# A gated attention block with a sign-weight FFN: squares of q and k folded to 64 rows before one turn, gates one step later

## The reference

```python
q, k, v = silu(xn @ Wq), silu(xn @ Wk), silu(xn @ Wv)
z, a, b = xn @ Wz, xn @ Wa, xn @ Wb
q, k, v = (causal_dwconv(t, w) for t, w in ...)     # 4 taps a channel
q, k = rope(q), rope(k)
q = q / maximum(norm(q), 1e-12); k = k / maximum(norm(k), 1e-12)   # over the 128 of a head
for s in range(4):
    attn = sum(q * lag(k, s)) / sqrt(128)
    out += (attn * sigmoid(lag(a, s) * b)) * lag(v, s)
s = (out * rsqrt(mean(out * out) + eps) * norm_w * silu(z)) @ Wout
hidden = relu((xn @ sign(up).T) * up_scale)
g = silu((hidden @ sign(down).T) * down_scale * output_scale)
y = x + s * g
```

## Time and profile before

| | us |
|---|---|
| median of 3 runs | 1365.18 (1363.66 to 1366.58) |
| the profiled execution | 1367.5 |
| its span in the trace | 1365.6 |
| PE busy in the span | 1342.8 (98%) |
| DVE busy | 985.0 (72%) |
| ACT busy | 745.5 (55%) |
| POOL busy | 361.6 (26%) |

### The profile page before, as it was taken

One profiled execution on the slowest core, in us unless ns is written; L12 is line 12 of the kernel. 1 busy time (PEld: TensorE's weight loads), 2 busy tenths in 40 slices (PEclk: granted clock), 3 DMA queues, 4 the chain that ended last, 5 costly groups with the idle time before them and its releaser, 6 DMA issues.

```text
span 1365.6 us, 23197 instructions
## 1 busy us (share of the span) xinstructions
PE 1342.8 (98%) x6824; PEld 1136.1 (83%) x6824; DVE 985.0 (72%) x1529; ACT 745.5 (55%) x2209; POOL 361.6 (26%) x508
## 2 busy tenths in 40 slices
PE   6999999999999999999999999998999999999998
PEld 5788888888888888888888888887888888888887
DVE  7898999989999899998999999995122223334432
ACT  5666666666666666566665666665543444432221
POOL 6134243343434333343333334333000000000001
PEclk9999999999999999999999999999999999999999
DMA  8233434334343433443433434335511101165544
GB/s 290 63 79 87 98 81 111 94 86 101 78 113 90 92 94 86 109 101 82 97 97 90 101 86 107 76 76 137 183 65 26 41 21 47 47 193 193 165 138 144
DMA packets 123419, 138.81 MB, mean 102 GB/s; under 512 B 30704, under 2 KB 67568, under 8 KB 123120
## 3 DMA queue, kind: packets, MB, share of 16 engines
q1 hardware_dynamic: 114160, 121.48, 31.1%
q0 software_dynamic: 9216, 16.78, 7.1%
HBM read 62.58 MB, written 25.30 MB: 64 GB/s over the span
## 4 chain that ended last, share of the span: by engine, by line
PE 96%; DMA 1%; DVE 1%; ACT 1%; POOL 1%; issue 0%; SPq 0%; POOLq 0%; DVEq 0%; ACTq 0%
PE bank L909 50%; PE bank L1411 12%; PE bank L1214 9%; PE bank L1201 8%; PE bank L962 4%; PE bank L984 4%; PE bank L973 4%; PE bank L950 2%; PE bank L899 1%; DMA sq_sum<-out_sq 1%; PE bank L886 0%; DMA up_raw<-in_x 0%; PE bank L925 0%; PE bank L117 0%; DVE y_k L753 0%
## 5 line engine op out<-in xcount | busy, mean ns | idle before, releaser
L645 ACT ACTIVATE bank<-bank 128x128 f32<-128x128 f32 x512 | 134.7, 263 | 92.1 <-PE bank L973 91.9
L753 DVE SCALAR_TENSOR_TENSOR y_q<-u_q,cw_q,y_q 128x512 f32<-128x512 f32 x192 | 144.2, 751 | 38.6 <-ACT y_q L610 31.1
L1190 DVE TENSOR_TENSOR hid_lo<-relu,hid_hi 128x512 fp32r<-128x512 f32 x64 | 44.3, 693 | 170.7 <-ACT hid_hi L1182 170.6
L753 DVE SCALAR_TENSOR_TENSOR y_k<-u_k,cw_k,y_k 128x512 f32<-128x512 f32 x192 | 145.2, 756 | 28.0 <-ACT y_k L610 21.1
L753 DVE SCALAR_TENSOR_TENSOR y_v<-u_v,cw_v,y_v 128x512 f32<-128x512 f32 x192 | 144.4, 752 | 6.9
L503 POOL TENSOR_TENSOR rq_win<-rq_win,const 128x32 f32<-128x32 f32 x64 | 27.5, 430 | 451.7 <-DMA rq_win<-rq_scratch 451.7
L487 POOL TENSOR_TENSOR rnorm<-norms,neg_half 128x8 f32<-128x8 f32 x64 | 111.9, 1749 | 9.9 <-POOL norms L483 8.9
L1178 ACT ACTIVATE relu<-bank,us_sb 128x512 f32<-128x512 f32 x64 | 44.1, 689 | 121.1 <-PE bank L1201 121.1
L1302 ACT ACTIVATE hid_hi<-o_raw 128x512 fp32r<-128x512 f32 x64 | 40.2, 630 | 115.9 <-PE bank L1411 97.0
L1362 DVE TENSOR_TENSOR hid_lo<-o_raw,hid_hi 128x512 fp32r<-128x512 f32 x64 | 43.8, 690 | 79.9 <-ACT hid_hi L1302 79.9
L1411 PE MATMUL bank<-x_hi,hid_hi 128*128 128x512 f32 x256 | 99.6, 389 | 0.0
(11 more groups left out here) (186 smaller groups left out, 3483.7 us busy)
## 6 DMA issues: line engine op xcount, KB each, us to landing
swapped_q<-y_q SPq DMA_DIRECT2D x128, 128.0 KB, 2.3
swapped_k<-y_k SPq DMA_DIRECT2D x128, 128.0 KB, 2.3
o_scratch<-o_buf SPq DMA_DIRECT2D x64, 256.0 KB, 2.5
sq_sum<-out_sq POOLq DMA_DIRECT2D x64, 256.0 KB, 3.4
o_raw<-o_scratch SPq DMA_DIRECT2D x64, 256.0 KB, 3.9
raw_q<-in_wq SPq DMA_DIRECT2D x16, 256.0 KB, 3.1
raw_k<-in_wk SPq DMA_DIRECT2D x16, 256.0 KB, 3.6
raw_v<-in_wv SPq DMA_DIRECT2D x16, 256.0 KB, 4.3
```

The source lines that it names most:

```text
L645: last = nc.scalar.activation(block_of, block_of, ACT.Square, accum_out=norms[:, g1 % 2, i * BC + b:i * BC + b + 1])
L753: nc.vector.scalar_tensor_tensor(y[n][:, g % 2, :], u[n][:, g % 2, i:i + CH], cw[n][:, bass.ds(h * TAPS + i, 1)], y[n][:, g % 2, :], ALU.m ...
L1190: nc.vector.tensor_tensor(hid_lo[:, j % HS, :], relu[:, j % 2, :], hid_hi[:, j % HS, :].bitcast(fp32), ALU.subtract).then_inc(hid_lo_done, 1)
```

## The change

The norms are made in another way. ACT squares q and k as they are, channels on the partitions: of q, rows 0 to 63 go into `fold` rows 0 to 63 and rows 64 to 127 into `other` rows 0 to 63; of k, in the same way, into rows 64 to 127. A transfer issued by POOL adds `other` to `fold`, so that 64 rows hold the squares of q and 64 those of k. PE turns `fold` alone, with four transposes, between the v and the z projection of the next step (`turn_fold`), and DVE sums each turned block over its two halves of 64 columns (`sum_fold`) into `norms`.

The fourth tap of v moves: DVE makes taps two and three, ACT makes the fourth as a scaled copy into `last_tap`, and a second accumulating transfer of POOL adds it to `y`. Only the very last step keeps the old way, and there DVE adds `other` to `fold` too.

`make_gates`, `gate_scores` and `mask_band` take the chunk of three steps before, not two, and the last two stand on DVE behind the taps of k, with `sum_fold` between them. `join_out` moves behind the rotation. POOL's step has the two new transfers first and the roots last. SP stores the roots behind the swaps. `fold`, `other` and `last_tap` lie in `down_raw`, so the FFN's first `down` weights are loaded after the last step instead of before the first. In the tail of the attention, the last two squares of the output get places of their own (`late_sq`), and the order of the work is another. The diff, cut to its core:

```diff
+    late_sq = [swapped["q"][:, i, :] for i in range(2)]
...
+    DVE_TAPS = {"q": 3, "k": 3, "v": 2}
+    last_tap = down_raw[:, 1, :, :]
+    fold, other = down_raw[:, 0, 0, :], down_raw[:, 0, 1, :]
...
-            if at := back(h, g, 1):
-                store_rq(at[1], c)
             for n in "qk":
                 wait(sp, conv_done[n], 3 * c + 3)
                 wait(sp, rope_done[n], 3 * (c - 1))
                 for to, frm in ((0, HALF), (HALF, 0)):
                     sp.dma_start(swapped[n][to:to + HALF, g % 2, :], y[n][frm:frm + HALF, g % 2, :]
                                  ).then_inc(swap_in[n][g % 2], 16)
+            if at := back(h, g, 1):
+                store_rq(at[1], c)
...
+        sp.wait_ge(turned_f, NC)
+        env["load_down"](sp, 0)
         store_rq(G - 1, NC)
-        load_rq(G - 2, NC)
-        load_rq(G - 1, NC, rq_last_in)
+        load_rq(G - 2, NC, rq_late_in[0])
+        sp.wait_ge(rq_joined, NC - 2)
+        load_rq(G - 1, NC, rq_late_in[1])
+        sp.wait_ge(last_tap_added, 16 * (NC - 1))
+        env["load_down"](sp, 1)
...
+        def add_last_tap(g1, c):
+            wait(pool, last_tap_made, c)
+            wait(pool, conv_done["v"], 2 * c)
+            wait(pool, turned_v, c - 1)
+            pool.sem_inc(last_tap_asked, 1)
+            nc.gpsimd.dma_start(y["v"][:, g1 % 2, :], last_tap[:, g1 % 2, :], accum_op=ALU.add
+                                ).then_inc(last_tap_added, 16)
+
+        def fold_squares(c):
+            wait(pool, squares_done, c)
+            pool.sem_inc(fold_asked, 1)
+            nc.gpsimd.dma_start(fold, other, accum_op=ALU.add).then_inc(folded, 16)
 
         def step(h, g):
             c = h * G + g
+            if at := back(h, g, 1):
+                fold_squares(c)
+                add_last_tap(at[1], c)
+            if at := back(h, g, 3):
+                make_gates(at[1], c - 3)
+            if at := back(h, g, 4):
+                add_squares(at[1], c - 4)
             if at := back(h, g, 1):
                 roots(at[0], at[1], c)
                 if is_start(h, g - 1):
                     pool.wait_ge(gate_done, 2)
                 gate_keys(at[0], at[1], c)
-            if at := back(h, g, 2):
-                make_gates(at[1], c - 2)
-            if at := back(h, g, 4):
-                add_squares(at[1], c - 4)
 
         schedule(pool, step)
...
+            if n == "v" and not is_end(h, g):
+                nc.scalar.activation(last_tap[:, g % 2, :], u["v"][:, g % 2, HALO:], ACT.Copy,
+                                     scale=cw["v"][:, bass.ds(h * TAPS + HALO, 1)]
+                                     ).then_inc(last_tap_made, 1)
...
-        def square_qk(g1, c):
-            wait(act, turned_qk, c)
-            wait(act, rnorm_done, c - 2)
-            for i, bank in enumerate((bank_tqv, bank_tk)):
-                for b in range(BC):
-                    block_of = bank[:, b * P:(b + 1) * P]
-                    last = nc.scalar.activation(block_of, block_of, ACT.Square,
-                                                accum_out=norms[:, g1 % 2, i * BC + b:i * BC + b + 1])
-            last.then_inc(norms_done, 1)
+        def squares(n, g, c):
+            own, far = (slice(0, HALF), slice(HALF, D)) if n == "q" else (slice(HALF, D), slice(0, HALF))
+            wait(act, conv_done[n], 3 * c + 3)
+            wait(act, turned_f, c)
+            nc.scalar.activation(fold[own, :], y[n][own, g % 2, :], ACT.Square)
+            last = nc.scalar.activation(other[own, :], y[n][far, g % 2, :], ACT.Square)
+            if n == "k":
+                last.then_inc(squares_done, 1)
...
-            if at := back(h, g, 1):
-                square_qk(at[1], c)
             if not is_start(h, g):
                 silu_and_tap("q", bank_qv, h, g, c)
                 silu_and_tap("k", bank_kz, h, g, c)
             if g == 3 and not is_last(h):
                 split_hi("q", h + 1, c)
+            squares("q", g, c)
...
                 ffn.up_signs(1)
+            squares("k", g, c)
...
-        square_qk(G - 1, NC)
         square_out(NC - 4)
         silu_z(G - 2, NC - 2, bank_kz)
         copy_v(G - 1, NC)
-        save_spill(G - 3, NC)
-        silu_z(G - 1, NC - 1, bank_qv)
-        ffn.down_signs(0)
-        ffn.down_signs(1)
         for n in "qk":
             act.wait_ge(rope_done[n], 3 * NC)
         ffn.hidden(0, 0)
+        save_spill(G - 3, NC)
+        silu_z(G - 1, NC - 1, bank_qv)
         square_out(NC - 3)
         ffn.hidden(0, 1)
+        ffn.down_signs(0)
         save_spill(G - 2, NC + 1)
         ffn.hidden(0, 2)
-        square_out(NC - 2)
+        square_out(NC - 2, late_sq[0])
+        ffn.down_signs(1)
+        save_spill(G - 1, NC + 2)
         ffn.hidden(0, 3)
-        save_spill(G - 1, NC + 2)
         act.wait_ge(o_done, NC)
         ffn.up_signs(2)
         ffn.down_signs(2)
-        square_out(NC - 1)
+        square_out(NC - 1, late_sq[1])
...
+        def sum_fold(g1, c):
+            wait(dve, turned_f, c)
+            wait(dve, root_done, c - 2)
+            nc.vector.tensor_reduce(norms[:, g1 % 2, :].rearrange("p (n b) -> p b n", b=BC),
+                                    bank_tk[:, :].rearrange("p (b n d) -> p b n d", b=BC, n=2),
+                                    AxisListType.X, ALU.add).then_inc(norms_done, 1)
...
+            if at := back(h, g, 3):
+                gate_scores(at[1], c - 3)
+            if at := back(h, g, 1):
+                sum_fold(at[1], c)
+            if at := back(h, g, 3):
+                mask_band(at[1], c - 3)
...
-            conv_tap("v", 3, h, g, c)
+            if is_end(h, g):
+                conv_tap("v", 3, h, g, c)
+                dve.wait_ge(squares_done, NC)
+                nc.vector.tensor_tensor(fold, fold, other, ALU.add).then_inc(folded_last, 1)
...
-            if at := back(h, g, 2):
-                gate_scores(at[1], c - 2)
             if at := back(h, g, 3):
+                join_out(at[1], c)
                 make_o(at[0], at[1], c - 3)
             if g == 1 and not (isinstance(h, int) and h == 0):
                 split_lo("z", h)
-            if at := back(h, g, 2):
-                mask_band(at[1], c - 2)
...
         def turn_v(g1, c):
-            wait(pe, norms_done, c)
-            wait(pe, conv_done["v"], 3 * c)
+            wait(pe, v_tok_done, c - 1)
+            if isinstance(c, int) and c == NC:
+                pe.wait_ge(conv_done["v"], 2 * NC + 1)
+            else:
+                wait(pe, last_tap_added, 16 * c)
...
-        def turn_qk(g1, c):
-            wait(pe, v_tok_done, c - 1)
+        def turn_fold(c):
             wait(pe, norms_done, c - 1)
-            for n, bank in (("q", bank_tqv), ("k", bank_tk)):
-                wait(pe, conv_done[n], 3 * c)
-                for b in range(BC):
-                    last = nc.tensor.transpose(bank[:, b * P:(b + 1) * P],
-                                               y[n][:, g1 % 2, b * P:(b + 1) * P], ident)
-            last.then_inc(turned_qk, 1)
+            if isinstance(c, int) and c == NC:
+                pe.wait_ge(folded_last, 1)
+            else:
+                wait(pe, folded, 16 * c)
+            for b in range(BC):
+                last = nc.tensor.transpose(bank_tk[:, b * P:(b + 1) * P], fold[:, b * P:(b + 1) * P], ident)
+            last.then_inc(turned_f, 1)
...
-            if at1:
-                turn_qk(at1[1], c)
...
+            if at1:
+                turn_fold(c)
...
-        turn_qk(G - 1, NC)
         wait(pe, z_done, NC - 2)
         project("z", bank_kz, H - 1, G - 2, NC - 2)
+        turn_fold(NC)
         turn_v(G - 1, NC)
         wait(pe, silu_done["v"], 2 * NC)
         project("z", bank_qv, H - 1, G - 1, NC - 1)
+        pe.wait_ge(norms_done, NC)
+        ffn.up(0, 0)
+        score(G - 2, NC - 2)
         sum_values(G - 3, NC)
-        score(G - 2, NC - 2)
-        ffn.up(0, 0)
         pe.wait_ge(z_done, NC - 1)
```

More of the change, by code:

```diff
@@ L294, in attention @@
     swap_in = {n: [sem(f"swap_in_{n}{i}") for i in range(2)] for n in "qk"}
-    turned_qk = sem("turned_qk")
+    squares_done = sem("squares_done")
+    fold_asked = sem("fold_asked")
+    folded = sem("folded")
+    folded_last = sem("folded_last")
+    turned_f = sem("turned_f")
     turned_v = sem("turned_v")
@@ L304, in attention @@
     rq_in = sem("rq_in")
-    rq_last_in = sem("rq_last_in")
+    rq_late_in = [sem(f"rq_late_in{i}") for i in range(2)]
     rq_masked = sem("rq_masked")
@@ L335, in is_start, with is_end @@
         return isinstance(h, int) and h == 0 and g == 0
+    def is_end(h, g):
+        return is_last(h) and g == G - 1
     def is_last(h):
@@ L498, in make_gates @@
             win = rq_win[:, g2 % 2, :, :]
[L499 to L500 removed]
+            if isinstance(k, int) and k >= NC - 2:
+                pool.wait_ge(rq_late_in[k - NC + 2], 16)
             else:
@@ L512, in make_gates, with add_squares @@
```

(17 more changed lines are left out.)

42 lines of the change are left out of this document (25 added, 17 removed).

## The result

The changed kernel takes 1354.16 us (median of 4 runs, 1352.64 to 1355.98); the kernel before, on the same chip, 1365.86 (4 runs, 1363.66 to 1366.58). The ratio is 0.9921 [0.9909, 0.9933]: 0.8% faster, where 1338 was forecast. The profiled execution took 1355.53 us, its span 1353.7, against 1367.5 and 1365.6.

The account below looks back on a forecast made before the run. PE, busy 98% of the span, was taken as the bound. 1367.5 - 27.9 (transposes) + 4 (mask waits) - 3.2 (end) - 1.5 (first steps) = 1338.9, or 1336.6 against the median; it said 1338, range 1330 to 1355.

Parts of the forecast that it names:

- The slack of an ordinary step: Mask before `sum_values` in an ordinary step: PE able to start at about 11.6, due at 11.89, keeping 0.3 us.
- 16 x 0.25 = +4 us: Step after g = 3: three weight splits make DVE's mask late, PE waits about 0.25 us in each of 16 heads.
- at worst 0.9: Gates' loop through POOL, SP and DRAM: ready at 20.7, due at 23.1; slack 2.4 us, 0.9 with the slowest landing.
- The first steps: Start of the attention: one wait of 1.6 for `v_tok` goes, as the fold's turn no longer opens the step; -1.5 us.
- The end: End of the attention: idle time and half clock, together 6.7 us, go; three short pauses, 3.5 together, come; net -3.2.
- no half clock expected: End of the attention: the new pauses, 3.5 us together, would be too short to lower PE's granted clock.
- The two other pauses that were expected: End of the attention: about 1 us for late gates after `up(0, 0)`, and some 0.5 at the last `sum_values`.
- The mask is late in every step: Rival, DVE in the loop: reduce or its waits cost 0.9 to 1.1, not 0.62; 1354 us at 1.0; chance 0.13.
- reduce slow: Rival, DVE's reduction: a strided read at half rate takes 1.3 us, giving 1377, slower than before; chance 0.05.
- The gates' loop becomes the period: Rival, POOL, SP and DRAM: two more transfers double every landing, the loop passes 14.05 us, kernel slower; chance 0.03.
- No wait at all: Rival, the loop: taps start earlier and PE never waits for the mask; 1333 us; chance 0.10.
- the rival whose cause was not at work: The late mask in every step, with a reduce of 1.0 us: 1354, to which the range was widened; chance 0.13.

Follow-up runs that it names:

- e3: Changed kernel with VectorE's reduction made twice, the first result to a tile nobody reads: 1379.82 us, ratio 1.0098 to the kernel before.
- e6: Changed kernel with VectorE's program written out for all 16 heads, same operations and order: 1347.75 us, ratio 0.9878 to the kernel before.
- e12: Kernel before the change with VectorE's program written out and nothing else: 1365.28 us, ratio 0.9993 to the kernel before.
- e4: Changed kernel with the transfer adding v's fourth tap cut to 16 of 512 columns: 1352.10 us, ratio 0.9899 to the kernel before.
- e8: Changed kernel with mask before the reduction, q's low weights made by GpSimd and join_out one operation earlier: 1344.35 us, ratio 0.9859.
- e5: Changed kernel with join_out one operation earlier, so a rotation operation stands between it and make_o: 1351.32 us, ratio 0.9903 to the kernel before.
- e1: Changed kernel with the mask ahead of the reduction on VectorE: 1349.72 us, ratio 0.9881 to the kernel before.
- e10: Changed kernel with mask before the reduction, join_out earlier and VectorE's program written out: 1341.28 us, ratio 0.9815 to the kernel before.
- e11: As e10, with ScalarE's first two FFN weight signs made after its last step: 1338.89 us, ratio 0.9803 to the kernel before.
- e7: Changed kernel with each of the fold's four transposes made twice, eight a step again: 1368.56 us, ratio 1.0029 to the kernel before.

## Why the prediction was wrong in size

The sign and the mechanism held; the gain came out at 11.7 us, not 27.

**What held.** A step of PE is 13.63 where nothing waits, by 0.44 for four turns. The reduction, which no row of before shows, was taken at the price of a PSUM copy. The instructions of DVE by line, changed kernel:

```profile
L831 DVE TENSOR_REDUCE norms<-bank 128x8 f32<-128x512 f32 x64 | 43.7, 683 | 2.1 <-PE bank L1036 2.1
```

683 ns, and 0.60 from start to start by e3; forecast 0.683 and 0.62. The lower bound was the value. Its rival from the Trainium skill's rule ("VectorE: DVE Perf Modes", "Rules for kernel authors"), a reduction that is the slowest operation of the engine, falls for this width: the trace has it level with the plain copy of the earlier trace rows and with the gate product, a `tensor_tensor` (0.70). The page's own tier table, which puts `tensor_reduce` at the 1x of `tensor_tensor`, agrees. The slack of an ordinary step was 0.31 (e3), forecast 0.3. In the loop PE waits neither for `folded` nor for the last tap: the two accumulating transfers are hidden, and so are ACT's work and POOL's.

**The step that failed: the term "16 x 0.25 = +4 us".** Its place is right, its size was 1.2 and not 0.25 (in 15 heads; head 0 has no g = 3 ahead of it). The forecast laid DVE's chain from the first tap of k at g = 3 to the mask of g = 0 with every operation starting right behind the one before. The timeline of DVE in the changed kernel, over just this chain:

```profile
525.52 2.33 DVE L798 SCALAR_TENSOR_TENSOR y_k<-u_k,cw_k,y_k 128x512 f32<-128x512 f32 x3 [0.44 <-ACT y_k L651]
528.07 0.71 DVE L839 TENSOR_TENSOR coef<-bank,gates 128x528 f32<-128x528 f32 x1 [0.21 <-POOL gates L534]
528.69 0.68 DVE L831 TENSOR_REDUCE norms<-bank 128x8 f32<-128x512 f32 x1
...
536.81 0.16 DVE L804 TENSOR_TENSOR bank<-bank,carry 128x8 f32<-128x8 f32 x1
537.19 0.75 DVE L856 SCALAR_TENSOR_TENSOR o_buf<-bank,nw_sb,z_act 128x512 f32<-128x512 f32 x1 [0.22 <-DVE bank L804]
537.86 0.74 DVE L798 SCALAR_TENSOR_TENSOR y_q<-u_q,cw_q,y_q 128x512 f32<-128x512 f32 x1
538.75 0.75 DVE L798 SCALAR_TENSOR_TENSOR y_q<-u_q,cw_q,y_q 128x512 f32<-128x512 f32 x1 [0.15 <-DVE y_q L798]
539.66 0.75 DVE L798 SCALAR_TENSOR_TENSOR y_q<-u_q,cw_q,y_q 128x512 f32<-128x512 f32 x1 [0.15 <-DVE y_q L798]
...
540.33 2.50 DVE L798 SCALAR_TENSOR_TENSOR y_k<-u_k,cw_k,y_k 128x512 f32<-128x512 f32 x3
542.74 0.70 DVE L839 TENSOR_TENSOR coef<-bank,gates 128x528 f32<-128x528 f32 x1
...
543.96 0.70 DVE L848 TENSOR_TENSOR coef<-coef,const 128x528 f32<-128x528 f32 x1
```

Piece by piece, from start to start:

| from, to | forecast | changed kernel | e6 |
|---|---|---|---|
| taps of k, gate product (g = 3) | 2.25 | 2.55 | 2.54 |
| gate product, `join_out` | 8.91 | 8.74 | 8.74 |
| `join_out`, `make_o` | 0.08 | 0.38 | 0.19 |
| `make_o`, taps of q | 0.66 | 0.67 | 0.67 |
| taps of q, taps of k (g = 0) | 2.25 | 2.47 | 2.26 |
| taps of k, gate product | 2.25 | 2.41 | 2.25 |
| gate product, mask | 1.24 | 1.22 | 1.21 |
| sum | 17.64 | 18.44 | 17.86 |

The chain is 0.80 longer; with 0.25 that is 1.05, and PE starts 0.94 behind the mask's start where 0.84 was taken. This makes the wait of 1.14 to 1.2 us a head. Two causes carry nearly all of it, each with its runs:

- *DVE's looped program, nearly 0.6.* The taps of q start 0.89 and 0.91 apart in place of 0.79, those of k take 0.16 longer, and `make_o` starts 0.38 behind `join_out`, whose result it reads. Written out (e6), these pieces shrink by 0.21 + 0.16 + 0.19 = 0.56, the step of g = 0 by the 0.58 from 14.83 to 14.25, and the loop by 8.0 us. The changed kernel shows the same by itself, since its loop ends ahead of the last head. There the taps of g = 0 stand as in e6:

```profile
871.80 2.37 DVE L798 SCALAR_TENSOR_TENSOR y_q<-u_q,cw_q,y_q 128x512 f32<-128x512 f32 x3
874.09 2.32 DVE L798 SCALAR_TENSOR_TENSOR y_k<-u_k,cw_k,y_k 128x512 f32<-128x512 f32 x3
```

`make_o` starts 0.19 to 0.21 behind `join_out` in the heads outside the loop and 0.29 to 0.42 in every step inside it. So not all of the pauses stand behind the branch; the one at `join_out` is ahead of it. Whether the branch or the addresses that hang on the loop's register cost the time isn't separated. In the kernel before the pauses cost nothing (e12), because its chain ended before PE asked; but they were in its trace (0.90 between taps), where the forecast took 0.79.
- *Gates that come late, 0.3.* At 528.07 the gate product waits for POOL; the chain starts with 2.55 for 2.25. The forecast let `rq_win` land in 2.0 and `make_gates` take 1.5, and so had 2.4 to spare, "at worst 0.9". SP's queue and the timeline of POOL in the changed kernel, for these gates:

```profile
521.68 0.57 SPq L402 DMA_DIRECT2D rq_win<-rq_scratch  x1
...
525.90 0.47 POOL L526 TENSOR_TENSOR rq_win<-rq_win,const 128x32 f32<-128x32 f32 x1 [3.56 <-DMA rq_win<-rq_scratch]
...
527.22 0.72 POOL L534 TENSOR_TENSOR gates<-rq_own,gate_k 128x16 f32<-128x16 f32 x1
```

From the start of the step before (504.61) the load is issued at 17.1, forecast 17.2. It lands 4.2 later, and `make_gates` takes 2.0: the gates are there at 23.3 in place of 20.7, where the gate product wanted them at 23.1. With the small transfer of e4 they are in time, and the step of g = 0 shortens by 0.23. In e6 the steps of g = 0 behind gates in time are about 0.3 shorter than the others.

Between `join_out` and `make_o` 0.11 of the 0.30 beyond the forecast is left in e6: `make_o`, which reads the result, starts 0.19 behind it, where the forecast took the 0.08 at which an operation that doesn't read it follows (e8: 531.50, 531.58). e5 puts another operation between the two and so takes away this and the loop's 0.19, for 4.6 us of the loop; its gain and that of e6 overlap.

The shares add up. Written out, and with the gates in time, a step of g = 0 takes 13.91 (e6), a wait of 0.28 beside the 0.25 of the forecast; with 0.3 for the gates and 0.58 for the loop this is 14.8, and 14.83 was measured. And e1, e5 and e6 together leave the loop at 805.08 (e10), within 1.5 us of no wait at all.

**The first steps: forecast -1.5, and nothing came.** The wait for `v_tok` is gone, but two of the same size are there: 1.7 for `u_v` before the third chunk's q projection, and 1.8 for the second fold. Its squares are ready at 61.7, but POOL, which issues its transfer, first waits for `gate`, which DVE makes once at the start:

```profile
65.25 0.65 POOL L515 TENSOR_TENSOR gate_k<-gate,rnorm 128x16 f32<-128x16 f32 x1 [3.07 <-DVE gate L913]
65.85 0.91 POOL L553 DMA_DIRECT2D down_raw<-down_raw  x1
```

The fold's turn starts at 69.34, 3.5 behind this issue. From the second q projection to the fifth PE took 89.09 - 47.08 = 42.01 before and takes 87.45 - 44.58 = 42.87 now. Neither wait was tried in an experiment.

**The end: forecast -3.2, -2.2 came.** The wait for the late z silu was right to 0.1 (2.1). But "no half clock expected" was wrong: behind this pause of 2.1 the granted clock is 0.63 over 4.6 us (0.50, the 1.2 GHz level, from 926 to 928), which costs 0.37 x 4.6 = 1.7. The two other pauses that were expected came to 0.4. Part of the gain shows only behind the first `down` matmul: before, the half-clock stretch reached to 959.20, 4 us into the FFN, and half of that is the 1.9 of the table's fourth row. e11 removes the pause, and with it the lower clock.

**The rivals.** "The mask is late in every step" and "reduce slow" fall by the 683 ns, though e3 shows that twice the price would indeed have lost. "The gates' loop becomes the period" falls by the ordinary steps of 13.63, but its mechanism, landings that double beside the new transfers, was real and cost a fifth to a quarter of the wait (e4, e6). "No wait at all" is what e10 had to be built for. The range, 1330 to 1355, held the time at its very end, and only because it reached to the rival whose cause was not at work: that was luck.

## What to carry to other kernels

When PE's step shortens, read the engine at 92% not by its mean but along its longest chain: at the step with extra work, with the hand-over behind short operations and the pauses of a looped program counted in, as the trace of before already shows them. Pauses that cost nothing before are the first to show when the pace rises; a run with the old pace restored (e7) tells such a cost from one that the change itself brings. Then put the result that the bounding engine waits for ahead of those that nobody waits for, and write out the follower's loop before moving its work to a neighbour.
